# Fused decoder layer on one core: attention stacks with lanes six rows apart instead of seven, rows of ones written by transfers

## The reference

```
q, k, v = split(x @ w_attn + b_attn)                      # one head, width 128
x = layernorm(x + (softmax(q k^T / sqrt(128) + causal mask) v) @ w_proj + b_proj)
q, k, v = x @ wq, ctx @ wk, ctx @ wv                      # 16 heads of width 8
bias[h, t, s] = rel_bias[bucket(s - t), h]
x = layernorm(x + (softmax(q k^T + bias) v) @ wo)
h = silu((x @ w1^T) * s1) * ((x @ w2^T) * s2)             # 128 -> 512
h = gelu((h @ h1^T) * t1); h = gelu((h @ h2^T) * t2)      # 512 -> 512, twice
x = layernorm(x + (h @ w3^T) * s3)
```

## Time and profile before

| what | value |
|---|---|
| median of 3 runs (lowest to highest) | 1088.15 us (1086.52 to 1097.75) |
| the profiled execution: its own time | 1093.1 us |
| its span, first to last instruction | 1091.3 us |
| its mean granted TensorE clock | 0.952 of full speed |
| busy: TensorE, VectorE, ScalarE, GpSimd | 969.3, 721.8, 605.5, 421.6 us |
| transfers | 156.10 MB, mean 143 GB/s |

### The profile page before, as it was taken

How to read it: one execution, slowest core, us unless ns; L and a number is a source line. 1 busy time by engine, 2 the same in 40 slices (tenths; PEclk the granted TensorE clock), 3 DMA queues, 4 the chain that set the end, 5 groups by cost and what they waited for, 6 DMA issues and landing times. The chain is left out here.

```text
span 1091.3 us, 25611 instructions
## 1 busy us (share of the span) xinstructions
PE 969.3 (89%) x10410; PEld 657.2 (60%) x10410; DVE 721.8 (66%) x1510; ACT 605.5 (55%) x1071; POOL 421.6 (39%) x418
## 2 busy tenths in 40 slices
PE   6754579999999999999999999989999988799996
PEld 3542256666666666666666666666666666545564
DVE  6565447878778877878778878876777774540014
ACT  2321157666667666666666666666666656352232
POOL 7330535554444555554444555554444400000000
PEclk9866689999999999999999999998999999899999
DMA  7507665555666655555665755554665420300000
GB/s 228 192 10 163 117 190 178 164 177 178 191 177 204 185 176 179 163 178 178 191 194 161 209 179 177 164 179 147 188 181 162 137 78 2 109 1 1 1 9 25
DMA packets 57388, 156.10 MB, mean 143 GB/s; under 512 B 23936, under 2 KB 36152, under 8 KB 54200
## 3 DMA queue, kind: packets, MB, share of 16 engines
q1 hardware_dynamic: 56744, 152.85, 48.1%
q10 hardware_dynamic: 528, 1.63, 0.4%
HBM read 111.63 MB, written 42.63 MB: 141 GB/s over the span
## 5 line engine op out<-in xcount | busy, mean ns | idle before, releaser
L769 ACT ACTIVATE e_sb<-st_ps 128x896 f32<-128x896 f32 (+1 forms) x384 | 354.1, 925 | 153.0 <-DVE st_ps L714 93.5
L108 DVE TENSOR_REDUCE cmax<-max_ps 112x1 f32<-112x512 f32 x512 | 337.6, 683 | 150.5 <-PE max_ps L98 150.4
L98 PE MATMUL max_ps<-kst,qst 111*112 111x512 bf16 x760 | 283.8, 401 | 37.8 <-PEq L117 14.1
L611 PEld LDWEIGHTS st_ps<-qst,kst 114*128 114x128 bf16 (+1 forms) x3072 | 191.7, 101 | 88.7 <-issue 41.8
L821 POOL TENSOR_TENSOR kpart<-k_left,kpart 128x500 bf16<-128x500 f32 x90 | 102.7, 1141 | 352.4 <-ACT k_left L787 347.8
L611 PE MATMUL st_ps<-qst,kst 114*128 114x112 bf16 (+1 forms) x3072 | 215.7, 213 | 19.5 <-DMA qst<-nmp 18.3
L105 DVE CUSTOM_DVE_ANT_0 near_out<-max_ps,near_nat 112x476 bf16<-112x476 f32 x248 | 154.0, 649 | 26.4 <-PE max_ps L98 26.4
L98 PEld LDWEIGHTS max_ps<-kst,qst 111*112 111x112 bf16 x760 | 92.2, 130 | 106.8 <-DVE cmax L108 38.9
L641 PE MATMUL pv_ps<-e_sb,vals 128*32 128x168 f32 (+1 forms) x3072 | 150.0, 313 | 0.3 <-ACT e_sb L769 0.3
L685 PEld LDWEIGHTS misc<-wv,ctxt 128*128 128x128 f32 (+1 forms) x768 | 99.6, 193 | 15.8 <-ACT vals L754 11.8
L641 PEld LDWEIGHTS pv_ps<-e_sb,vals 128*32 128x32 f32 (+1 forms) x3072 | 80.4, 109 | 47.1 <-issue 34.6
(11 more groups left out here) (127 smaller groups left out, 941.1 us busy)
## 6 DMA issues: line engine op xcount, KB each, us to landing
kst<-kparts SPq DMA_DIRECT2D x192, 375.0 KB, 6.2
kparts<-kpart SPq DMA_DIRECT2D x90, 375.0 KB, 2.7
ctxt<-in_ctxT SPq DMA_DIRECT2D x32, 750.0 KB, 7.4
qst<-qslots SPq DMA_DIRECT2D x192, 28.0 KB, 6.4
qslots<-qst SPq DMA_DIRECT2D x4, 672.0 KB, 11.2
kparts<-kst SPq DMA_DIRECT2D x6, 375.0 KB, 3.1
h<-in_h SPq DMA_DIRECT2D x2, 1024.0 KB, 8.6
qst<-nmp SPq DMA_DIRECT2D x96, 1.8 KB
```

The lines of the kernel that those rows point to most:

```text
L98: return nc.tensor.matmul(dst[0:TT, 0:hi - lo], m.qst[0:M_ROW, r, p, :], m.kst[0:M_ROW, r, p, lo:hi], start=True, stop=True)
L108: return nc.vector.tensor_reduce(m.cmax[:, r, c, p:p + 1], src[0:TT, 0:BOUND[c + 1] - BOUND[c]], AX.X, ALU.max)
L611: mm = nc.tensor.matmul(st_ps[0:K, j % 2, p // 4, (p % 4) * TT:(p % 4 + 1) * TT], m.kst[0:AUG, u % RING, p, j * P:j * P + K], m.qst[0:AUG, ...
L769: nc.scalar.activation(e_sb[0:K, j % E_RING, :].rearrange("p (a c) -> p a c", a=2), st_ps[0:K, j % 2, :, 0:HALF], ACT.Exp).then_inc(s_ex, 1)
```

## The change

Lanes are six rows apart, so that no row is spare: `M_ROW` becomes 96 and `AUG` 99, `max_scores` contracts over 96 rows and the scores over 99, and `stack_rows` steps by six. The memsets of whole buffers of `kst` go. A tile `ones` of 3 x 1500 is set on VectorE; SyncE writes it to rows 96 to 98 of buffers 0 and 1 (3 partitions x 48,000 bytes), and at the start of cross-attention copies those rows of buffer 0 to buffer 2 (3 partitions x 24,000 bytes).

```diff
-STEP = SLOTS + 1
 LANES = 2 * DH
-M_ROW = STEP * LANES - 1
+M_ROW = SLOTS * LANES
 AUG = M_ROW + 3
...
 def stack_rows(slot, first=0, lanes=LANES):
-    return slice(STEP * first + slot, STEP * (first + lanes - 1) + slot + 1, STEP)
+    return slice(SLOTS * first + slot, SLOTS * (first + lanes - 1) + slot + 1, SLOTS)
...
-        eps = sb("eps", [TT, 1])
+        eps, ones = sb("eps", [TT, 1]), sb("ones", [3, S], BF16)
...
             sp.dma_start(m.x1[:, :, :], d["x"].rearrange("(i p) c -> p i c", p=TT)).then_inc(s_xn, 16)
 
+            sp.wait_ge(s_on, 1)
+            sp.dma_start(m.kst[M_ROW:AUG, 0:SA_K, :, :].rearrange("k r p s -> k (r p) s"),
+                         ones[:, :].unsqueeze(1).broadcast_to([3, SA_K * PAIRS, S])).then_inc(s_kz, 16)
+
...
-                sp.wait_ge(s_kz, n + 1)
+                sp.wait_ge(s_kz, 16)
                 stack_k(sp, d, m, n, m.s_kl[n])
...
             nc.gpsimd.memset(m.near_nat[:, :, NEAR:FIRST_CH], 0.0).then_inc(s_mem, 1)
-            nc.gpsimd.memset(m.kst[:, 1, 0:PAIRS // 2, :], 1.0)
...
-                    pool.wait_ge(s_kz, 1)
-                    nc.gpsimd.memset(m.kst[:, 1, PAIRS // 2:PAIRS, :], 1.0).then_inc(s_kz, 1)
                     pool.wait_ge(s_xb, 2)
...
             nc.vector.tensor_copy(u_sb[:, :], ps[0:H, 5, 0:URANGE]).then_inc(s_ue, 1)
-            nc.vector.memset(m.kst[:, 0, :, :], 1.0).then_inc(s_kz, 1)
+            nc.vector.memset(ones[:, :], 1.0).then_inc(s_on, 1)
...
         def _(pool):
-            for g in range(NG):
-                pool.wait_ge(m.s_qd[g], 16 * 6)
-            for h in range(2):
-                ins = nc.gpsimd.memset(m.kst[:, SA_K, h * PAIRS // 2:(h + 1) * PAIRS // 2, :], 1.0)
-                ins.then_inc(s_kz, 1)
             pool.wait_ge(s_own, 16)
...
                     if u + 2 == SA_K:
-                        sp.wait_ge(s_kz, 2)
+                        sp.wait_ge(s_kz, 16)
...
             for g in range(NG):
                 sp.wait_ge(m.s_qd[g], 16 * 6)
+            sp.dma_start(m.kst[M_ROW:AUG, SA_K, :, :], m.kst[M_ROW:AUG, 0, :, :]).then_inc(s_kz, 16)
             sp.dma_start(m.wo[:, :, :], d["wo"]).then_inc(m.s_wo, 16)
```

More of the change, by code:

```diff
@@ L152, in self_attention_block @@
         s_ur, s_u, s_ue, s_ud, s_un, s_nt, s_nte = (sem(n) for n in ("ur", "u", "ue", "ud", "un", "nt", "nte"))
-        s_kz, s_mem, s_xg = (sem(n) for n in ("kz", "mem", "xg"))
+        s_kz, s_on, s_mem, s_xg = (sem(n) for n in ("kz", "on", "mem", "xg"))
         s_qz = [sem(f"qz{g}") for g in range(NG)]
```

## The result

The changed kernel takes 1097.51 us in the median of 20 runs (1091.42 to 1104.76); the kernel before, run beside it, 1087.69 us (1084.61 to 1097.75, 20 runs). The ratio of the two is 1.0086, with a 95% interval from 1.0067 to 1.0104. The change makes the kernel 0.9% slower. I had forecast 1086.6 us, no measurable difference; 1097.5 lies within the range of 1079 to 1101, but the time moved the other way.

A forecast was written before the change was run, and what follows sets the result against it. TensorE, 95% busy, was taken to bound the cross-attention loop, a chain through all engines the part before. Only VectorE's memset counted, -1.5 us, all else 0: 1088.15 - 1.5 = 1086.65, so 1086.6 us; range 1079 to 1101.

The forecast's parts named there:

- the slower rival: Cross-attention loop: denser stacks land later and TensorE waits; 7.5 to 31.5 us, middle 19.5, giving 1106.1 us; chance 0.13.
- a margin of 1.1 to 1.9 us: Cross-attention loop: time between the last query transfer's landing and TensorE's first matmul on these stacks; none in two iterations.
- My signs of being wrong: Line 98's wait 0.3 us an iteration, key landing well over 6.2, shorter matmuls, or self-attention ending over 4 us from 112.5.
- the price: Later stacks in the loop: 0.25 to 1.05 us an iteration over thirty stacks, 7.5 to 31.5 us, middle 19.5.
- the quarter that I put on 8.6 us: Six key transfers of a stack, 8.6 us, priced a quarter longer with lanes over 96 partitions: 2.15 us.
- The head: Self-attention and the start of cross-attention, before the loop: without VectorE's memset the chain through all engines gains 1.5 us.
- the sum: Self-attention: first `v` at 11.67, 5.97 us earlier, of which collisions of VectorE with GpSimd leave 1.5 us.
- the division starts near 23.2 under line 250 and ends near 26.1: VectorE's line 461 in self-attention, ending 26.1 instead of 30.57; the next subtraction then falls under line 255, shrinking the gain.
- The bound of -13.5 us: Most that self-attention could gain: the full 5.97 us plus line 479's 7.49 us gone from the chain.
- the most is 0.63 us: SyncE's issue of the two transfers of ones: both covered at cost 0, at most 0.63 us each, once.
- GpSimd's memsets: Lines 242, 259 and 807: removal worth 0; for line 807, at most 3 us once if its cover were gone.
- fewer rows: Matmuls over 96 and 99 rows instead of 111 and 114: no shorter, worth 0.

The follow-up runs named there:

- experiment 1: The kernel before with one line changed: lanes of a stack six rows apart instead of seven, memsets and contracted rows kept; 1103.14 us, ratio 1.0139.
- experiment 2: The changed kernel with lanes seven rows apart again, ones written by transfer to the 16 spare rows and rows 112 and 113; 1082.5 us, ratio 0.9946 against the kernel before.
- layout from row 0: The changed kernel with slots 0 to 3 in rows 0 to 63, lanes four apart, slots 4 and 5 in rows 64 to 95, two apart; 1108.69 us.

## Why the prediction was wrong

**The step that failed is the forecast that the denser stacks cost nothing,** that is, the weight given to the slower rival: 0.13, "that nothing in this trace shows the place of the partitions to matter". The argument was sound as far as it went; the trace of one layout can't show another. But that was absence of evidence, and I counted it as evidence against. What stood on the other side was strong: a full DMA stretch (93%) and a margin of 1.1 to 1.9 us that was empty in two iterations. Two facts on one side and a silence on the other do not make 0.13. The term that I had put at nothing measured 15.6 us (experiment 1).

My signs of being wrong said so: the wait came to 0.45 us an iteration (13.5 us over 30) against 0.3, the key stack's landing to 7.3 us against 6.2, and the block of self-attention ended 5.0 us from 112.5.

**The rival's mechanism was right and its size roughly so.** Named were the place (line 98's first matmul in step 8, behind the last query transfer), the price (7.5 to 31.5 us) and the sign to look for. Measured: the spacing alone costs 15.6 us (experiment 1), the middle of the price had been 19.5. The landing rises by 1.1 us for the key and 1.6 us for the query transfers, and the last of them lands 1.4 us later after the first issue (17.1 against 15.7), where I had 2.15 for the stack. That the price came near is in part luck, for two reasons. The pattern was another, as told below. And the quarter that I put on 8.6 us was an estimate of mine that no row and no run shows; the 1.4 us that the runs showed in its place are a sixth of 8.6.

**The pattern** was not as I had it, 0.25 to 1.05 us in each of 30 iterations: there are 9 waits of 0.2 to 2.6 us and none between, in iterations 50 to 77 us apart from 360 to 760 us and further apart outside that. Why these iterations and not the others is open. Three of the nine:

```profile
359.50 0.61 PE L97 MATMUL max_ps<-kst,qst 96*112 96x476 bf16 x2 [0.58 <-DMA qst<-qslots]
...
410.17 0.61 PE L97 MATMUL max_ps<-kst,qst 96*112 96x476 bf16 x2 [1.92 <-DMA qst<-qslots]
...
487.09 0.61 PE L97 MATMUL max_ps<-kst,qst 96*112 96x476 bf16 x2 [2.42 <-DMA qst<-qslots]
```

The other wait, for the maxima in `qst`, fell from 18.3 to 14.7 us in total at the same time, so the two together grew by 8.4 us, near the 7.6 us that the loop became longer in this execution.

**The head was mis-sized: -1.5 us forecast, -6.5 measured at the end of self-attention.** `v` started at 12.47, near the 11.7 of the sum. The first subtraction ended at 20.32, under GpSimd's first split, as laid out. The step that failed is the next: "the division starts near 23.2 under line 250 and ends near 26.1". It started at 22.24. GpSimd's chain, which I had held fixed, had itself moved later by 0.7 us at its start (16.81 against 16.12) and by 1.0 at its third instruction (23.29 against 22.32): TensorE's value matmuls ran 3.14 us instead of 1.97, and ScalarE's copies, which release it, came later. So the division fell under GpSimd's second instruction, which ends at 23.21, and was through at 23.69, and the second group's subtraction got ahead of the addition of `bproj` instead of under it. The bound of -13.5 us held it; a margin of one microsecond on either side of a collision should have stopped me from taking one point. Of the 6.5 us, 3.3 were given back by the start of the loop.

**The issue of the ones was mis-sized too:** it took 6.84 us, against "the most is 0.63 us":

```profile
10.03 6.84 SPq L193 DMA_DIRECT2D kst<-ones  x1
```

The first key stack was issued 3.2 us later than before (33.51 against 30.29), and this cost nothing only because nothing waited for it: the query stores still began 8.0 us earlier.

**Right:** GpSimd's memsets cost nothing that can be told from the noise, both transfers are covered, and fewer rows don't make a matmul shorter: between 150 and 875 us the maxima's matmuls of 512 columns have a mean of 395 ns over 96 rows and 396 ns over 111. The margin of the stacks was the right thing to measure.

## What to carry to other kernels

When a change moves where transfers write, measure the slack behind their last landing first. If it is a fraction of the landing time and the DMA engines are nearly full (93% here), treat a slower landing as likely until a run of the new placement says otherwise. Separate a layout from what rides along with it: here the memsets' removal was worth 5 us (experiment 2) and the denser rows cost 15.6 (experiment 1), and together they looked like one loss of 0.9%. And look at the granted clock behind a long wait, for the row of waits doesn't hold what it costs: here the clock stood at 0.50 for 3.4 us behind waits of 1.92, 2.57 and 2.39 us.

## What the runs showed of the hardware that was not expected

Equal transfers at other partitions (four moved by 32, two by 64) changed the time of the kernel by 1.7% (1108.69 against 1089.9 us) and the DMA engines' share from 48.6% to 53.5%. From six apart to the layout from row 0 that share rose only by 0.3 points and the median landing by 0.2 us (7.3 to 7.5), while the time rose by 11.2 us: the loop ran 30.7 us at the lower clock instead of 10.2.

The granted clock fell to 0.50 for 3.4 or 6.8 us at some long waits of TensorE in the loop, and not at others. For the query stack: it fell at a wait of 1.48 us (6.8 us, layout from row 0) and at those of 1.92 and 2.57 us (3.4 us each, changed kernel), and not at one of 2.42 us in the changed kernel. For the maxima: it fell at 2.52 us (6.8 us) and at 1.64 us (3.4 us) in the kernel before, and not at 1.91 us in experiment 2.

A memset of 128 x 12000 on VectorE took 10.06 us (GpSimd was at a memset of its own beside it until 10.38), that of 3 x 1500 took 1.31 us and that of 16 x 1500 in experiment 2 also 1.31: 16 rows took as long as 3, and eight times the columns, over 128 rows, took 7.7 times as long.
